# One normalisation's stages and an activation table's load placed elsewhere in a four-layer transformer kernel on one Trainium2 core

## The reference, cut to what matters

```python
# layer 0, attention block: post-normalised; its third normalisation closes the block
x = x + _L0_xattn_ref(_layernorm(x), ctx)        # ends with _ln(r + lin2(relu(lin1(r))), ln3_g, ln3_b)
x = x + _L0_ffn_ref(_layernorm(x), w_switch, ...)  # router: argmax expert of 8, capacity, relu expert
...
# layer 2, expert part: top 2 of 8 experts with a capacity
x = x + _L2_xattn_ref(_layernorm(x), ctx, ...)
x = x + _L2_ffn_ref(_layernorm(x), w_g, c_fc, c_proj)
# layer 3
x = x + _L3_xattn_ref(_layernorm(x), ctx, ...)
x = x + _L3_ffn_ref(_layernorm(x), router_w, ...)
```

## Time and profile before

| | us |
|---|---|
| median of 3 runs | 570.28 |
| lowest, highest | 567.09, 572.21 |
| the profiled execution | 568.02 |
| its span, first to last instruction | 566.2 |

### The profile page before, as it was taken

One profiled execution on the slowest core, in us unless ns is written; L12 is line 12 of the kernel. 1 busy time (PEld: TensorE's weight loads), 2 busy tenths in 40 slices (PEclk: granted clock), 3 DMA queues, 4 the chain that ended last, 5 costly groups with the idle time before them and its releaser, 6 DMA issues. The chain is left out here.

```text
span 566.2 us, 9171 instructions
## 1 busy us (share of the span) xinstructions
PE 488.0 (86%) x3277; PEld 389.7 (69%) x3277; DVE 325.7 (58%) x1142; ACT 242.0 (43%) x479; POOL 237.5 (42%) x343
## 2 busy tenths in 40 slices
PE   2699895779878986997388799999899999999997
PEld 2658475659565644685278499998554887899997
DVE  4766617864796842678862255544767854433334
ACT  2562735315145650334671263421743395234340
POOL 4791775545427010367677535572840430000000
PEclk9899898569857998996579999999999799999999
DMA  9999720311680028900111222116300000000002
GB/s 280 335 207 209 215 103 1 105 31 37 208 272 2 0 70 199 291 1 0 33 53 50 81 81 66 40 34 219 87 2 1 1 1 0 1 1 1 1 1 75
DMA packets 56861, 48.04 MB, mean 85 GB/s; under 512 B 6082, under 2 KB 47240, under 8 KB 56688
## 3 DMA queue, kind: packets, MB, share of 16 engines
q1 hardware_dynamic: 53728, 42.06, 26.9%
q0 software_dynamic: 2656, 4.88, 2.7%
q10 hardware_dynamic: 432, 0.52, 0.4%
HBM read 35.21 MB, written 12.82 MB: 85 GB/s over the span
## 5 line engine op out<-in xcount | busy, mean ns | idle before, releaser
L2138 DVE SCALAR_TENSOR_TENSOR x<-ps,gate,x 128x128 f32<-128x128 f32 x128 | 36.1, 344 | 54.8 <-PE ps L1282 54.8
L1282 PEld LDWEIGHTS ps<-moe_w,big 128*128 128x128 f32 x512 | 61.1, 192 | 3.9 <-issue 1.7
L1557 ACT ACTIVATE big<-ps,col 128x512 f32<-128x512 f32 x64 | 42.2, 688 | 48.2 <-PE ps L1095 48.1
L1282 PE MATMUL ps<-moe_w,big 128*128 128x128 f32 x512 | 61.4, 275 | 0.9 <-DVE x L2127 0.9
L2499 POOL DMA_INDIRECT res<-qT,dest x43 | 42.2, 983 | 37.3 <-DVE qT L2113 23.3
L727 PE MATMUL ps<-con,xn 128*128 128x128 f32 x148 | 29.9, 338 | 26.8 <-ACT xn L1490 15.4
L727 PEld LDWEIGHTS ps<-con,xn 128*128 128x128 f32 x148 | 21.2, 174 | 37.1 <-DVE xn L1698 33.8
L1218 PE MATMUL ps<-moe_w,big 128*128 128x128 f32 x344 | 41.1, 275 | 0.6 <-ACT big L1549 0.6
L2298 POOL TENSOR_SCALAR rstd<-mv 128x4 f32<-128x4 f32 x33 | 8.5, 258 | 78.8 <-DVE mv L1683 78.0
L1218 PEld LDWEIGHTS ps<-moe_w,big 128*128 128x128 f32 x344 | 39.8, 192 | 0.8 <-ACT big L1549 0.8
L1402 ACT ACTIVATE xT<-ps 128x512 f32<-128x512 f32 x37 | 21.7, 589 | 41.2 <-PE ps L727 41.2
(11 more groups left out here) (362 smaller groups left out, 1182.5 us busy)
## 6 DMA issues: line engine op xcount, KB each, us to landing
ring<-in_ew SPq DMA_DIRECT2D x20, 256.0 KB, 5.1
moe_w<-in_m0w SPq DMA_DIRECT2D x16, 256.0 KB, 6.1
moe_w<-in_m2w SPq DMA_DIRECT2D x16, 256.0 KB, 5.3
tok<-zero SPq DMA_DIRECT2D x1, 2580.0 KB, 27.6
big<-tok SPq DMA_DIRECT2D x7, 322.5 KB, 3.0
res<-zero SPq DMA_DIRECT2D x1, 2048.0 KB, 28.9
moe_w<-in_ew SPq DMA_DIRECT2D x8, 256.0 KB, 5.5
big<-res SPq DMA_DIRECT2D x4, 512.0 KB, 5.1
```

The lines of the kernel that those rows point to most:

```text
L1282: last = mm(ps[7 - i % 2 if i >= B else 6 + i % 2][:, cols(c)], big[:, FC * (e % 2) + f, i % B, cols(c)], w[:, e, F + P * f:F + P * f + P] ...
L1557: A(big[:, 2 * (e % 2) + f, t, :], bank[:, :], ACT.Gelu, bias=V("m3b1", 2 * e + f)).then_inc(h_act, 1)
L2138: last = v.scalar_tensor_tensor(out=x[:, C * t + c, :], in0=bank[:, cols(c)], scalar=gate[:, C * t + c, e:e + 1], in1=x[:, C * t + c, :], ...
```

## The change

It has five parts.

1. The empty stage "gain" is taken out of SEQ0, so that stats x3 of a tile stands one step earlier.
2. In four steps around it (LOW_FIRST) DVE, ACT and POOL take the tiles from the lowest up, PE from the highest down as before. The scale of x3 is signalled through `rstd_ready` (its target for later normalisations is two higher), no longer through `nm_ready` and `tok_act`.
3. In the normalisation for the router of layer 0 ACT takes three of the four chunks of tiles 0 to 2, and DVE one.
4. In layer 2's router, tile 0's deviation goes the way of the other tiles: square root on ACT, reciprocal on DVE, between DVE's logits sum and its choice of the expert. POOL's four instructions for it are gone.
5. Two table loads are asked for earlier: the square root's right behind layer 2's last exponential, the exponential's right behind layer 3's last query projection.

```diff
-        ("stats", "out", "r"), ("scale", "x3"), ("gain",), ("stats", "x3", "x"), ("scale", "xn"),
+        ("stats", "out", "r"), ("scale", "x3"), ("stats", "x3", "x"), ("scale", "xn"),
...
+DOWN = SEQ0.index(("down",))
+LOW_FIRST = range(DOWN - 1, DOWN + 3)
...
+ROW_NORM = NORM_X3 + 1
+def act_share(k, t):
+    return ACT_SHARE + (k == ROW_NORM and t < B - 1)
...
-def skewed(stages, seq, late=None):
+def skewed(stages, seq, late=None, rising=()):
...
         order = list(reversed(range(B)))
+        if step - B + 1 in rising:
+            order = order[::-1]
...
+                    if name == "L3q" and t == B - 1:
+                        act.preload_act_table_set("exp_and_others")
...
+                    if name == "L2" and t == B - 1:
+                        act.preload_act_table_set("sqrt_and_others")
...
-                    act.wait_ge(nm_ready, 4 * k + t + 1)
-                    for c in range(C * t + (C - ACT_SHARE if where == "xn" else 0), C * t + C):
+                    if where == "x3":
+                        act.wait_ge(rstd_ready[t], NORM_X3 + 1)
+                    else:
+                        act.wait_ge(nm_ready, 4 * k + t + 1)
+                    for c in range(C * t + (C - act_share(norm, t) if where == "xn" else 0), C * t + C):
...
-            scaled(0)
-            for t in range(1, B):
+            for t in range(B):
                 tt = slice(C * t, C * t + C)
                 act.wait_ge(var_ready[t], SENT_NORM)
                 A(spread[:, tt], mv[:, tt, 1], ACT.Sqrt, bias=eps[:, :]).then_inc(root_ready, 1)
-                rows_turned(t - 1)
+                if t:
+                    rows_turned(t - 1)
                 scaled(t)
...
                     link(i)
+                    if between:
+                        between(t)
                     first_largest(lg[:, chunks(t), :], oh[:, chunks(t), :], chunks(t))
...
-                dve.wait_ge(root_ready, t)
+                dve.wait_ge(root_ready, t + 1)
...
-            choose_(0)
+            choose_(0, deviation)
...
-            deviation(0)
```

More of the change, by code:

```diff
@@ L123 @@
 ROW_TURN = sum(q[0] == "turn" for q in SEQ0) - 1
-ROW_SCALE = sum(q[0] == "scale" for q in SEQ0) - 1
+ROW_SCALE = sum(q[0] == "scale" and q[1] != "x3" for q in SEQ0) - 1
 LAST_TURN = sum(q[0] == "turn" for q in SEQ0 + SEQ1 + SEQ2 + SEQ3) - 1
@@ L159, in skewed, with wavefront @@
                 stages[step - t](t)
-def wavefront(make, seq, late=None):
-    skewed(staged(make, seq), seq, late)
+def wavefront(make, seq, late=None, rising=()):
+    skewed(staged(make, seq), seq, late, rising)
 SQUARES = [("L0v", 128), ("L0so", 128), ("L0q", 128), ("L0k", 128), ("L0mv", 128), ("L0o", 128),
@@ L562, in build, with rstds @@
         SENT_NORM = sum(q[0] == "stats" for q in SEQ0 + SEQ1 + SEQ2)
+        def rstds(k):
+            return k + 2 * (k > NORM_X3)
         def soft(name, t):
@@ L963, in scale @@
             def scale(where):
-                n["normed"] += 1
+                n["normed"] += where != "x3"
             def count(name):
@@ L1439, in stage @@
                     act.wait_ge(s_max[t], smax)
-                    act.wait_ge(rstd_ready[t], norm)
+                    act.wait_ge(rstd_ready[t], rstds(norm))
                     for q in range(C):
@@ L1482, in scale @@
                 k, norm = n["scale"], n["norm"]
-                n["scale"] += 1
+                n["scale"] += where != "x3"
                 src = r if norm in (2, 3, NORM_X3) else x
@@ L1487, in stage @@
                 def stage(t):
-                    act.wait_ge(nm_ready, 4 * k + t + 1)
-                    for c in range(C * t + (C - ACT_SHARE if where == "xn" else 0), C * t + C):
+                    if where == "x3":
[3 more added lines that the diff above has]
+                    for c in range(C * t + (C - act_share(norm, t) if where == "xn" else 0), C * t + C):
                         last = A(dst[:, c, 0:D], src[:, c, :], ACT.Identity, bias=negmean[:, c:c + 1], scale=rstd[:, c:c + 1])
-                    last.then_inc(tok_act, 1)
+                    last.then_inc(rstd_ready[t] if where == "x3" else tok_act, 1)
                 return stage
@@ L1585, in _ @@
             act.wait_ge(ld_c, 32)
-            wavefront(make, SEQ0)
+            wavefront(make, SEQ0, None, LOW_FIRST)
             placed("m0", 0, ACT.Relu, "m0b1")
@@ L1695, in stage @@
                 def stage(t):
-                    dve.wait_ge(rstd_ready[t], k)
-                    for c in range(C - ACT_SHARE):
+                    dve.wait_ge(rstd_ready[t], rstds(k))
+                    for c in range(C - act_share(k, t)):
                         i = v.tensor_scalar(dst[:, C * t + c, 0:D], src[:, C * t + c, :], mv[:, C * t + c, 0:1],
@@ L1811, in choose, with stage @@
                 out_k = n["out"]
-                def stage(t):
+                def stage(t, between=None):
                     dve.wait_ge(out_mm, 4 * out_k + t + 1)
@@ L2141, in experts @@
                     last.then_inc(y_used, 1)
-            wavefront(make, SEQ0, "mix")
+            wavefront(make, SEQ0, "mix", LOW_FIRST)
             rows_of()
@@ L2527, in _ @@
             skewed(stages[:CHOICE], SEQ2)
-            _, deviation, _, sent_away, _ = stages[CHOICE:]
-            deviation(0)
+            sent_away = stages[CHOICE + 3]
             for t in range(B):
```

11 lines of the change are left out of this document (5 added, 6 removed).

## The result

| | median us | lowest to highest | runs |
|---|---|---|---|
| the kernel before, beside it | 568.87 | 567.09 to 572.21 | 18 |
| the changed kernel | 565.06 | 562.42 to 567.44 | 18 |

The ratio is 0.9932, with a 95% interval of 0.9917 to 0.9948: 3.8 us or 0.7% less, between 3.0 and 4.7 us. The forecast was 3.8 less, at 566.5, and within 1%; the median lies 1.4 under that, as the kernel before ran at 568.87 here and not at 570.28. The profiled execution took 565.77 us, with a span of 564.0.

The account below looks back on a forecast made before the run. DVE, POOL and ACT in turn were taken to bound the end of layer 0's attention, where PE idles. Gains of 3.2 + 0.6 + 0 = 3.8 us against a median of 570.28 gave 566.5, range 562.0 to 570.4.

Parts of the forecast that it names:

- What sets the pace: End of layer 0's attention: DVE, POOL and ACT in turn set the pace while PE idles 8.47 us.
- The walk through DVE's new queue: Layer 0's router normalisation: step-by-step times of DVE's reordered sums and x3 stages, priced from the trace, giving 3.2 us.
- Part A: Layer 0's router normalisation: empty stage removed, lowest tile first, three chunks on ACT; 3.2 us gained.
- the mark: PE's turn of tile 3 for layer 0's router, forecast to move from 109.42 to 106.2.
- Part B: Layer 2's router: tile 0's deviation off POOL starts the first send 0.6 us sooner, limited by the slots.
- Part C: Table loads moved earlier, ahead of layer 2's tile 0 root and layer 3's exponentials: nothing gained.
- What it gains, the rest gains: Behind tile 3's turn in layer 0 the order is unchanged, so the 3.2 us gained there carry through.
- Rival 1: Layer 0's x3 stages: POOL's root blocks DVE, up to 0.9 us each for tiles 1 and 2; gain 2.0; 15%.
- Rival 2: POOL not stretched in layer 0, slots not later in layer 2: gain 5.4 us, 564.9; 13%.
- Rival 3: Layer 0: the wait moves to tile 3 through extra POOL or ACT work; gain under 1.5 us, about 569.5; 9%.
- Rival 6: The change doesn't do what it says, by a second load or a hiding order: no difference, 570.3; 4%.
- Rivals 4 and 5: PE's clock at layer 0's experts returns later, 572.5 us at worst, 6%; or falls better, 563 us, 7%.

Follow-up runs that it names:

- The experiment with this part alone: Kernel before with only the third normalisation changed (empty stage gone, lowest tile first, three chunks on ACT): 565.41 us, ratio 0.9947.
- A kernel with the mark 1.40 sooner: The whole change with the highest tile first again in the four steps: 569.07 us, ratio 0.9996.
- one with 1.61: The whole change with the empty stage put back, order and shares kept: 568.07 us, ratio 0.9997.
- the probe: The whole change plus unused work at its end, POOL powers and additions beside DVE statistics and additions; DVE's additions took 0.67 to 0.68 us beside powers.
- the kernel with tile 3's row split: The whole change with tile 3's normalised row scaled half on DVE, half on ACT: 562.96 us, ratio 0.9893.
- 35 or 40 fillers: Unused PE matmuls: 35 added to the whole change with tile 3's row split, 566.46 us; 40 to the whole change with highest tile first, 568.60 us.

## Why the prediction was right

- **What sets the pace (right).** DVE, POOL and ACT in turn, then one chain from tile 3's turn on. The walk through DVE's new queue held to 0.25 us at every point of the table above.
- **Part A, 3.2: right, 2.99 at the mark.** The 0.2 are a price that was too small: the 2.70 from statistics to ACT's scaling came from a root whose first POOL instruction took 0.58. On tile 3's root it took 0.79 now, and the way from the statistics (96.65) to ACT (99.60) was 2.95. The prediction puts the whole stretching down to that first instruction, but the second's 0.64 was in the 2.70 too. The experiment with this part alone gives 3.0 in time.
- **Part B, 0.6: right.** 4.56 to 3.96 at the send, through the slots (+0.55, forecast +0.5) and not through ACT's scaling, which came 1.18 sooner (forecast 1.25). In time it is 0.3 to 2.6.
- **Part C, 0: right,** by the experiment without the early loads. What the sum didn't say is that part B rests on the first load: 0.48 of its 0.60 at the send. ACT's next instruction starts 0.01 behind the load's end in both kernels and in the experiment (265.58, 265.40), so the 1.38 us of draining that the Trainium skill, "ScalarE: Activation LUTs", section "What ACT_TABLE_LOAD costs", adds to each switch don't show here; by them the first copy behind the load would have started near 266.95.
- **"What it gains, the rest gains": this was the weak step.** It holds for the change, by the medians, but not because the rest is moved as a whole. A kernel with the mark 1.40 sooner, and one with 1.61, gave it all back by L1233, since PE's clock came back 51 instead of 44 us after the sum. In them too PE's work behind the mark was moved as a whole until the clock parted them, which is what the prediction had named against such a loss. So it was partly luck that this step held.
- **Rival 1 (DVE blocked), 15%: wrong.** DVE's operations of the x3 stages took 0.66 to 0.69, and the probe shows it for powers that had started first. The Trainium skill, "SBUF — State Buffer", section "SBUF: two separate sides", has a lock for the whole instruction, whoever starts first; for this power of 128x4 on POOL the measurement speaks against it. Where DVE's operation started first the trace agrees with the rule: POOL's short operations beside DVE's go from 0.23 to 0.58 to 0.79, and end 0.08 to 0.09 behind DVE's.
- **Rival 2: no;** both its terms were at the forecast's value. **Rival 3: no:** ACT's tile 3 started at 99.60, 0.1 past the bound that I had set, but 0.67 of that is this execution's lateness. **Rival 6: no.**
- **Rivals 4 and 5 (the clock), 6 and 7%: not here, though real.** The clock came back 40.7 us after the sum instead of 44.0, 3.3 sooner where the mark was 3.0 sooner. Rival 4 happened in the two kernels that have only the order or only the stage's removal. Its chance was too small: of the three distances at which the mark stood, about 27.4, 28.9 and 30.4, the middle one meets it.

**Open:** what decides when the clock comes back. The returns stood at 40.5, 44.0 and 51 us, not in the order of the mark (26.7 to 28.0, 30.4, 28.8 to 29.0), and closing most of the short pauses right ahead of the experts didn't change it. Each of the six kernels with a mark up to 27.95 and no fillers had the first, both with 28.8 to 29.0 the last. These are single executions, so a return may also differ from one execution of a kernel to the next.

## What to carry to other kernels

Where four engines hand tiles on, walk the new queue of the fullest engine with the durations of the trace, the stretched ones where two engines lie beside each other: that gave every point to a quarter of a microsecond. A stage without instructions isn't free if it is a step of a skewed order, and neither is the order within a step; here each, left out, cost about half of the gain at the mark. A gain ahead of a stretch that PE bounds must be checked again behind the next rise of PE's clock, by the length of the same matmuls on both sides; keeping PE busy with fillers held the clock up at first, and on the kernel with tile 3's row split lost more behind it than it gained.

## What was not expected of the hardware

PE's clock, once low, came back 23.9, 27.3 or 34.1 us later (by the trace's record, in the kernels without fillers ahead of the router), with the work in between nearly the same; between 27.3 and 34.1 lie 1.8 to 1.9 us, by the same PE instructions on both sides. With 35 or 40 fillers the fall came 13.9 or 13.5 us later, and the low stretch lasted 17.1 or 10.2 us.

A POOL instruction of 0.23 us that lay beside a DVE addition or multiplication from two operands in SBUF ended 0.08 to 0.09 us behind it, while a power that had started first left DVE's additions at their 0.67 to 0.68.
